# A selective-scan block on one core: chunks 13 and 15 exchange their kinds

## The reference

```python
z = einsum(mz, Wc) + bc                       # one for each direction
dlt, Bm, Cm = split(z @ Wdbc.T)
delta = softplus(dlt @ Wdt.T + bdt)
h[t] = exp(delta[t] * A) * h[t-1] + delta[t] * Bm[t] * z[t]     # for each e and n
y[t] = sum over n of h[t, e, n] * Cm[t, n] + z[t] * Dp
out = x + gate * ((silu(mx) * (y1 + y2)) @ Wf.T + bf + skip)
```

## Time and profile before

| | |
|---|---|
| median of 3 runs | 3278.92 us (3277.81 to 3281.28) |
| profiled execution, its own time | 3282.95 us |
| its span | 3281.1 us |
| VectorE (DVE) busy | 3014.0 us, 92% |
| TensorE (PE) busy | 2988.6 us, 91% |
| GpSimd (POOL) busy | 2900.1 us, 88% |
| ScalarE (ACT) busy | 2679.4 us, 82% |
| scans, L1322 | 1024 in three groups, means 2.264 to 2.276 us |
| VectorE's products with C, L1331 | 320, 1.221 us each |
| POOL's products with C, L1235 | 704, 2.378 us each |
| mean granted clock of TensorE | 0.985 |

### The profile page before, as it was taken

The page is one execution under the profiler, slowest core; times in us unless marked ns, Lnnn a source line. Parts: engine busy times, 40 slices in busy tenths (PEclk is TensorE's granted clock), DMA queues, the critical chain, the costliest instruction groups (busy, mean ns, idle before and its releaser), DMA issues.

```text
span 3281.1 us, 54891 instructions
## 1 busy us (share of the span) xinstructions
PE 2988.6 (91%) x19924; PEld 2373.0 (72%) x19924; DVE 3014.0 (92%) x2006; ACT 2679.4 (82%) x5153; POOL 2900.1 (88%) x1280
## 2 busy tenths in 40 slices
PE   8978999899998999899999999899999999899999
PEld 5756666667767666678877766678778666677789
DVE  2739999999999999999999999999999999999994
ACT  1448999988888999987788999987877999988772
POOL 0428999999999999999999999999998999999993
PEclk9989999999999999999999999999999999999999
DMA  5765334644475333645575434645566333645463
GB/s 223 248 230 187 130 119 135 225 160 156 167 250 198 132 130 127 224 151 157 162 246 186 135 118 137 222 140 165 167 217 209 122 131 130 228 137 165 155 199 111
DMA packets 207053, 560.40 MB, mean 171 GB/s; under 512 B 20200, under 2 KB 66472, under 8 KB 202560
## 3 DMA queue, kind: packets, MB, share of 16 engines
q1 hardware_dynamic: 203424, 538.01, 48.9%
q10 hardware_dynamic: 2208, 10.49, 0.9%
q0 software_dynamic: 1152, 8.39, 0.6%
HBM read 476.19 MB, written 80.63 MB: 170 GB/s over the span
## 4 chain that ended last, share of the span: by engine, by line
PE 50%; ACT 20%; DVE 12%; issue 10%; DVEq 0%; ACTq 0%
PE y L880 14%; PE slot L891 10%; PE mb L851 9%; ACT abuf L1129 8%; PE mb L964 6%; DVE hbuf L1322 6%; ACT slot L1191 3%; DVE hbuf L1331 3%; PE mb L861 3%; PE slot L903 3%; DVE slot L1322 3%; ACT dec L1191 2%; ACT soft L1085 2%; PE mb L922 1%; PE mb L957 1%
## 5 line engine op out<-in xcount | busy, mean ns | idle before, releaser
L1235 POOL TENSOR_TENSOR hbuf<-hbuf,cres 128x1024 f32<-128x1024 f32 x704 | 1664.6, 2378 | 143.4 <-DVE hbuf L1322 143.4
L1230 POOL TENSOR_TENSOR bst<-bst,du 128x1024 f32<-128x1024 f32 x512 | 1221.0, 2385 | 46.3 <-DVE du L1266 46.3
L1322 DVE TENSOR_TENSOR_SCAN hbuf<-dec,slot 128x1024 f32<-128x1024 f32 x512 | 1164.9, 2275 | 39.0 <-PE slot L903 27.1
L880 PE MATMUL y<-ident,hbuf 128*128 128x128 f32 x8192 | 1016.1, 273 | 0.0
L880 PEld LDWEIGHTS y<-ident,hbuf 128*128 128x128 f32 x8192 | 924.5, 141 | 104.5 <-issue 104.0
L1129 ACT ACTIVATE abuf<-dut,bt 128x128 f32<-128x128 f32 x3072 | 964.5, 387 | 0.0
L1322 DVE TENSOR_TENSOR_SCAN slot<-slot,bst 128x1024 f32<-128x1024 f32 x320 | 728.3, 2276 | 23.0 <-ACT slot L1191 22.1
L1191 ACT ACTIVATE slot<-delta,par 128x1024 f32<-128x1024 f32 x512 | 568.2, 1110 | 198.1 <-DVE hbuf L1331 185.1
L1191 ACT ACTIVATE dec<-delta,par 128x1024 f32<-128x1024 f32 x512 | 584.1, 1141 | 115.5 <-DVE hbuf L1322 114.9
L891 PE MATMUL slot<-ident,abuf 128*128 128x128 f32 x3072 | 408.4, 276 | 170.4 <-ACT abuf L1129 161.0
L891 PEld LDWEIGHTS slot<-ident,abuf 128*128 128x128 f32 x3072 | 339.0, 141 | 302.8 <-ACT abuf L1129 243.9
(11 more groups left out here) (156 smaller groups left out, 2363.2 us busy)
## 6 DMA issues: line engine op xcount, KB each, us to landing
bst<-bc_s SPq DMA_DIRECT2D x512, 512.0 KB, 4.0
cres<-bc_s SPq DMA_DIRECT2D x128, 512.0 KB, 6.8
wzs<-wz_s SPq DMA_DIRECT2D x64, 256.0 KB, 4.1
yf_s<-yrd SPq DMA_DIRECT2D x32, 512.0 KB, 5.3
ybuf<-yf_s SPq DMA_DIRECT2D x32, 512.0 KB, 4.9
yg_s<-ybuf SPq DMA_DIRECT2D x31, 512.0 KB, 4.4
si_s<-silu SPq DMA_DIRECT2D x28, 512.0 KB, 6.1
silu<-si_s SPq DMA_DIRECT2D x28, 512.0 KB, 5.4
```

The lines of the kernel that those rows point to most:

```text
L880: last = nc.tensor.matmul(y[:, j * P:(j + 1) * P], hbuf[:, q % HR, j * P:(j + 1) * P], ident[:], start=False, stop=(q % N == N - 1), is_tr ...
L1230: nc.gpsimd.tensor_tensor(bst[:, i % BR, :], bst[:, i % BR, :], du[:, k % 2, :], ALU.mult).then_inc(pool_b, 1)
L1235: nc.gpsimd.tensor_tensor(hbuf[:, q % HR, :], hbuf[:, q % HR, :], cres[:, q % N, :], ALU.mult).then_inc(pool_prod, 1)
L1322: nc.vector.tensor_tensor_scan(h[:, ::step], decays[:, ::step], inflows[:, ::step], 0.0, ALU.mult, ALU.add).then_inc(scanned, 1)
```

## The change

In every unit chunk 13 becomes a V chunk and chunk 15 a P chunk. Nothing else is edited; `kind`, `before` and the tables built on them follow. The chunks that are V or P are the same ones together, so the inflows, their places in POOL's queue, SP's loads of B and everything of the A and E chunks stay the same. What follows from the kinds: scan 13 writes into the slot and scan 15 into `hbuf`; VectorE's product stands behind scan 13, ahead of what else its queue has at step 13, and no longer behind scan 15; POOL has no product at step 14 and has that of chunk 15 at step 0 of the next unit; who waits for the one or the other waits for the other engine.

```diff
-KINDS = "EVAVEVAPAVAPAPAV"
+KINDS = "EVAVEVAPAVAPAVAP"
 SCALE_STEPS = {0: ((2, 0), (2, 1)), 3: ((6, 0),), 5: ((6, 1),), 6: ((8, 0),), 7: ((8, 1),), 8: ((10, 0),),
```

## The result

| | before | after |
|---|---|---|
| median | 3280.10 us (4 runs) | 3327.97 us (4 runs, 3322.71 to 3330.65) |
| ratio | | 1.0144, 95% interval 1.0130 to 1.0158 |
| profiled execution, its own time | 3282.95 us | 3327.95 us |
| span | 3281.1 us | 3326.2 us |

The change makes the kernel 47 us slower (0.0144 x 3280); 3327 was forecast. (The median of before has one run more than the one shown above.)

What follows compares the result with a forecast made beforehand. VectorE, 97% busy, was taken to set the pace through its waits at unit handovers. Terms of 34.3 (27 gating), 14.0 (28 mx) and 0 (8 others) sum to 48.3 us on 3278.92: forecast 3327, range 3306 to 3339.

Steps and rivals of the forecast that it cites:

- The tie at the turn of du: 27 gating handovers: du completes as TensorE reaches it, so the later du delays scan 0 by 1.27 us each, 34.3 total.
- The freed product at chunk 15 gains nothing: Gating handovers: no product behind scan 15 only lengthens scan 0's wait for the spread, from 0.56 to about 1.83 us.
- ScalarE's 0.50: 28 handovers of units computing mx: decay 15 waits for chunk 13's product, sigmoid and scan 1 start 0.50 later, 14.0 us.
- The eight others: Handovers where batch or direction changes: the later product fits existing waits, so 0, up to 1.2 us either way each.
- The pace is the work: Rival: VectorE's work, not the order, sets the time, which stays at 3279, give or take 3; chance 0.04.
- One term is covered: Rival: only the gating term (3313) or only the mx term (3293) costs time, the other is covered; chance 0.12.
- The clock falls: Rival: TensorE's added idle in 27 gating units lowers its clock; if in a quarter, about 38 us more, 3366; chance 0.07.
- VectorE is released early: Rival: at chunk 0, without the product behind scan 15, scan 0 starts earlier and idle time closes, 3253; chance 0.03.

Runs made afterwards that it cites:

- e1: Kernel before with the exchange of kinds only in the 31 units that gate; 3312.98 us, ratio 1.0092.
- e3: Kernel after, but in gating units VectorE does the second half of du ahead of chunk 13's product; 3295.21 us, ratio 1.0039.
- e11: Kernel before, kinds untouched, with the second half of du in gating units one scan later, behind scan 14; 3358.34 us, ratio 1.0237.
- e6: Kernel before with chunk 15 as a P chunk whose POOL product is one column wide; 3282.17 us, ratio 1.0001.
- e2: Kernel before with the exchange of kinds only in the 33 units that don't gate; 3296.15 us, ratio 1.0042.
- e12: e3 with VectorE's product of chunk 13 done for one column of 1024 only; 3282.05 us, ratio 0.9996.
- e7: e3 with ScalarE's decay 1 written between the two groups of scalings; 3280.35 us, ratio 0.9997.
- e4: Kernel before with ScalarE's decay 1 between its two groups of four scalings, save in 8 units; 3264.84 us, ratio 0.9947.
- e9: e3 with decay 15 written into the SBUF tile of C's row 15, not loaded; chunk 15 takes C's row 14; 3377.83 us, ratio 1.0293.

## Why the prediction was right

*The tie at the turn of du.* It rested on the earlier trace rows: du complete within 0.05 us of TensorE's arrival, and nothing that gives the delay back. Forecast 1.27 for each of 27, measured 1.25 in all but one. e1 has the term alone, e3 takes it away by swapping two instructions, e11 makes it larger by the length of a scan.

*The freed product at chunk 15 gains nothing.* The wait at scan 0 was forecast at 1.83 and is 1.79 (1.65 in the units of batch 0, where it was 0.41). e6 shows it in its purest form.

*ScalarE's 0.50.* Forecast 0.50 in each of 28 with a wait of 0.88 at scan 1, measured 14.0 us in all and 0.84. e2 has it alone, e12 takes it away. Two points of the working were less good than the sum. The lateness does not end at scan 1, as e7 showed. And that the sum is met to the tenth is luck: the wait itself is 28 x 0.46 = 12.9, and the rest comes from spreads for chunk 4 at a lower clock, which stand in both kernels. One of them, unit 18 of the kernel after:

```profile
1099.46 3.55 PE L903 MATMUL slot<-diag,dut 128*128 128x128 f32 x16 [1.16 <-DVE hbuf L1322]
1103.11 2.29 DVE L1322 TENSOR_TENSOR_SCAN hbuf<-dec,slot 128x1024 f32<-128x1024 f32 x1 [0.34 <-PE slot L903]
```

The granted clock is 0.53 over this spread. In unit 19 the same 16 matmuls, behind the same 1.16 us of idle time, take 2.02 at 1.00. Of the 24 spreads for chunk 4 in the units 2 to 7, 18 to 23, 34 to 39 and 50 to 55, 11 are slow (2.97 us or more) in the trace after and 4 in the trace of before. So some of the 28 handovers cost up to 1.0, and the handovers at the ends of units 34, 49, 52 and 56 cost -0.06 to 0.15, since the spread in the unit behind them was slow in the kernel before. TensorE also has a new idle time of 0.54 us ahead of L840 in these 24 units. Whether this makes slow spreads more frequent isn't shown: e2 has it and 11 of them, e3 9, but e1, e6 and e11 without it have 6, e12 8 and e4 none.

*The eight others.* Put at 0, they give -1.7: +1.4 at the end of unit 31, +0.8 at 15, -1.9 at 47, the rest between -1.0 and 0. At 15, 31 and 47 scan 15 no longer waits 0.94 for its decay, and the next scan 0 waits otherwise than before: 1.76 where it waited for nothing, 3.67 for 1.28 and 4.27 for 5.14. At 31 and 47 TensorE waits for something ahead of the projection that isn't du; the load of its tokens would fit, but no run tried it. These two move without the change as well: e4 leaves them alone and has +0.5 and -2.6. At 7, 23, 39 and 55 gain and loss nearly cancel, as the prediction says: scan 15 waits 0.31 for 1.37, scan 1 1.06 for 0.57, and scan 0 has a new wait of 0.29 for decay 0.

*The rivals.* "The pace is the work" is refuted by e6 and by the result; the Trainium skill's rule of the busiest engine (Perfetto Trace Analysis, Identifying the Most-Contended Engine) named VectorE, and 76 us less of its work behind scan 15 brought nothing. "One term is covered" is refuted by e1 and e2. "The clock falls" did not happen at the 27 places: behind the wait of 1.03 us the granted clock stays at 1.00 (1550 to 1566 us, for one), and 26 of the handovers differ from before by the same 1.24 to 1.26. It does happen in mx units, as said above, and e11 shows it for a wait of 1.9. "VectorE is released early" is refuted at scan 0.

## What to carry to other kernels

Ask of a moved instruction not how long its engine is busy but who waits for what stands behind it in its queue: 1.2 us of product cost nothing behind scan 15 and 1.25 us ahead of du. An engine that is 97% busy can still have its slack in one place and none a few microseconds earlier; find where each chain ties, as with du and TensorE's turn. When a late engine feeds several others in order, repairing the first wait only shows the next one, so go back to where the lateness begins.

## What the runs showed of the hardware

- A scan on VectorE with both inputs in SBUF took 4.86 us on average beside a busy POOL, against 2.26 with one of them in PSUM, and POOL's products 2475 ns against 2378 (e9). The Trainium skill (SBUF — State Buffer, Who interferes with whom) has a VectorE instruction with two SBUF inputs contend with a GpSimd instruction that reads SBUF, and calls the port pair that they share an exclusive lock. The trace of e9 agrees. In unit 3 the scan starts at 434.74, POOL's inflow ends at 436.98, and the scan ends 2.15 later; POOL's next product takes 4.41 us. In unit 4 the scan takes 6.70, past the ends of two of POOL's instructions, and POOL's next starts 0.15 behind the scan's end.
- The same 1.9 us of idle time ahead of the same matmuls was followed by 2.4 GHz in 15 handovers and by a stretch at 1.2 GHz in 12 (e11); 1.03 us of it was followed by full speed throughout the gating handovers (after). The 1.16 us ahead of the spread for chunk 4 were followed by 2.4 GHz in 13 mx units and by a stretch at 1.2 GHz in 11 (after).
- A VectorE instruction that doesn't wait starts about 0.09 us before its predecessor's record ends, so a wait costs that much more than the idle time in its row (e4).
